# Filler products in five places of TensorE, one value product moved in the attention loop, one memset moved

## The reference

```python
x = x + L0_xattn(layernorm(x), ctx)   # 16 heads of 16 channels, softmax over the 361 context rows
x = x + L0_ffn(layernorm(x))          # shared FFN plus top-2 of 8 experts, 1024 hidden channels
x = x + L1_xattn(layernorm(x), ctx)   # linear layers with ternary weights and int8 inputs, two attention units
x = x + L1_ffn(layernorm(x))          # gated cell scanned over the 16 batches, then tanh of a product
```

```python
attn = softmax(clip(q @ k.T * scale))
x    = (attn @ v) @ Wo + bo
```

## Time and profile before

| What | us |
|---|---|
| median of 3 runs | 918.67 (918.64 to 931.78) |
| the profiled execution, device time | 917.04 |
| its span, first to last instruction | 915.1 |
| TensorE busy | 775.8 |
| VectorE busy | 702.4 |
| ScalarE busy | 557.9 |
| GpSimd busy | 291.6 |
| mean granted TensorE clock | 0.927 of full |

### The profile page before, as it was taken

One profiled execution on the slowest core, in us unless ns is written; L12 is line 12 of the kernel. 1 busy time (PEld: TensorE's weight loads), 2 busy tenths in 40 slices (PEclk: granted clock), 3 DMA queues, 4 the chain that ended last, 5 costly groups with the idle time before them and its releaser, 6 DMA issues.

```text
span 915.1 us, 21761 instructions
## 1 busy us (share of the span) xinstructions
PE 775.8 (85%) x8198; PEld 584.1 (64%) x8198; DVE 702.4 (77%) x1455; ACT 557.9 (61%) x1156; POOL 291.6 (32%) x256
## 2 busy tenths in 40 slices
PE   3788999999998677899899999996647998869995
PEld 1456666666665464778477777783224886459994
DVE  7767888888888897876667776647886987767766
ACT  6657767677674346543655556646977775763542
POOL 6244544535442524050522220005721221532400
PEclk9789999999999778999999999999558999789997
DMA  6434444445543356242477766532210000200002
GB/s 174 109 75 101 118 100 108 108 107 125 140 106 90 94 189 227 90 128 58 125 200 192 197 194 175 151 89 60 74 37 1 1 1 10 85 0 3 3 1 72
DMA packets 75661, 89.60 MB, mean 98 GB/s; under 512 B 22069, under 2 KB 62276, under 8 KB 75584
## 3 DMA queue, kind: packets, MB, share of 16 engines
q1 hardware_dynamic: 68752, 80.50, 31.9%
q0 software_dynamic: 6144, 7.42, 3.3%
q10 hardware_dynamic: 688, 0.66, 0.3%
HBM read 72.87 MB, written 15.43 MB: 97 GB/s over the span
## 4 chain that ended last, share of the span: by engine, by line
PE 50%; DVE 20%; ACT 9%; issue 8%; POOL 6%; DMA 5%; SPq 1%; DVEq 0%; ACTq 0%; POOLq 0%
PE ps L1213 11%; PE ps L1200 9%; PE ps L575 4%; PE ps L547 3%; PE ps L475 3%; PE ps L528 3%; ACT area L1738 2%; PE ps L377 2%; PE ps L619 2%; PE ps L2298 2%; DVE p L563 2%; PE ps L2309 2%; PE ps L1814 2%; ACT area L1705 1%; DVE m L533 1%
## 5 line engine op out<-in xcount | busy, mean ns | idle before, releaser
L533 DVE TENSOR_REDUCE m<-ps 100x2 f32<-100x722 f32 x128 | 114.9, 899 | 48.1 <-PE ps L528 46.8
L554 ACT ACTIVATE p<-ps 128x800 f32<-128x800 f32 x128 | 106.6, 833 | 47.6 <-PE ps L547 45.7
L1262 ACT ACTIVATE hT<-ps,cols 128x500 f32<-128x500 f32 (+1 forms) x96 | 62.5, 651 | 96.6 <-PE ps L1200 85.8
L563 DVE SCALAR_TENSOR_TENSOR p<-p 128x600 f32<-128x600 f32 x128 | 106.1, 829 | 1.0 <-ACT p L554 1.0
L1213 PE MATMUL ps<-w_h,hT_h 128*125 128x256 f16 (+1 forms) x384 | 104.7, 273 | 1.8 <-DVE x L1309 1.2
L1213 PE MATMUL ps<-w_h,hT_l 128*125 128x256 f16 (+1 forms) x384 | 104.7, 273 | 0.0
L1213 PE MATMUL ps<-w_l,hT_h 128*125 128x256 f16 (+1 forms) x384 | 104.7, 273 | 0.0
L1269 DVE TENSOR_TENSOR hT_l<-hT,hT_h 128x500 f16<-128x500 f32 (+1 forms) x96 | 62.4, 652 | 54.6 <-ACT hT_h L1263 54.3
L1105 POOL DMA_INDIRECT xe<-tokens,slot_of x32 | 44.4, 1387 | 146.3 <-PE ps L1223 99.0
L1200 PE MATMUL ps<-xe_h,w_h 128*128 128x500 f16 (+1 forms) x192 | 71.4, 372 | 16.0 <-ACT hT_h L1263 6.2
L1200 PE MATMUL ps<-xe_l,w_h 128*128 128x500 f16 (+1 forms) x192 | 71.1, 370 | 0.0
(11 more groups left out here) (356 smaller groups left out, 2099.7 us busy)
## 6 DMA issues: line engine op xcount, KB each, us to landing
stage<-in_ctxT_dram SPq DMA_DIRECT2D x16, 541.5 KB, 6.2
sw<-in_L_ffn_w_dram SPq DMA_DIRECT2D x16, 512.0 KB
sw<-in_L_ffn_w_dram SPq DMA_DIRECT2D x8, 1024.0 KB, 5.9
k_parts<-kp SPq DMA_DIRECT2D x32, 192.0 KB, 3.9
ks<-k_parts SPq DMA_DIRECT2D x32, 192.0 KB
stage<-in_L_xattn_W_f_dram SPq DMA_DIRECT2D x6, 1024.0 KB, 7.7
ctx_f<-in_ctxT_dram SPq DMA_DIRECT2D x16, 270.8 KB, 3.1
ks<-k_parts SPq DMA_DIRECT2D x32, 96.0 KB
```

What stands on the lines that cost most here:

```text
L533: v.tensor_reduce(m32[p][:, 2 * i:2 * i + 2], ps[0:T, at:at + 2, 0:KV], AX.X, ALU.max).then_inc(m_max, 1)
L554: s.activation(p32[:, i % HALF, :, :, :].rearrange("p j n t -> p n j t"), ps[:, t_bank(i):t_bank(i) + 2, 0:(KJ + 1) * T].rearrange("p n (j ...
L563: v.scalar_tensor_tensor(probs, probs, 1.0, low, ALU.min, ALU.max).then_inc(a_cv, 1)
L1262: s.activation(hT[:, f % 3, 0:m], bank[2 + f % 2][:, 0:m], ACT.Silu, bias=bias, scale=1.0 / WS)
```

## The change

A new function issues n products into a PSUM bank that nobody reads before the next product starts it afresh. It is called in five places: ahead of the first key product; ahead of block f = 2 of the first hidden layer; after the turned layer norm of the third sublayer; after its attention units; and between F1 and F2. In the attention loop, `v_tensor` of step 1 goes ahead of the wait for `m_l` and of `pv_tensor(b - 1, q, 3)`, and `pv_tensor(b, p, 1)` with its wait goes from step 5 to step 6. In the opening, the memset of rows 64 to 127 of the key tile goes behind the first layer norm, and SyncE stores the first keys before it waits for that memset.

```diff
+        def keep_running(pe, at, weights, moving, n):
+            for i in range(n):
+                pe.matmul(at[:, 0:moving.shape[1]], weights, moving, start=True, stop=True)
...
+                if i == 1 and has(b, 2):
+                    v_tensor(pe, b + 1, q, 0, (k_32, 2 * b + 5))
                 if i == 1:
                     pe.wait_ge(m_l, 2 * b + 2)
                 if i == 1 and from_(b, 1):
                     pv_tensor(pe, b - 1, q, NQ - 1)
-                if i == 1 and has(b, 2):
-                    v_tensor(pe, b + 1, q, 0, (k_32, 2 * b + 5))
...
-                if i == 5 and has(b, 1):
+                if i == 6 and has(b, 1):
                     pe.wait_ge(m_l, 2 * b + 3)
-                if i == 5:
+                if i == 6:
                     pv_tensor(pe, b, p, 1)
...
             ln_tensor(pe, 2)
+            pe.wait_ge(ln_ev, 2 * (B // 2) + 1)
+            keep_running(pe, bank[0], w_q[F1][:, 0, 0:128], w_q[F1][:, 1, 0:512], 10)
...
             att_tensor(pe, 1)
+            keep_running(pe, bank[2], w_q[F1][:, 0, 0:128], w_q[F1][:, 1, 0:512], 18)
...
+            pe.wait_ge(h_ev, 8 + 4 * FC - 7)
+            keep_running(pe, bank[0], w_q[F1][:, 0, 0:128], w_q[F1][:, 1, 0:512], 20)
             pe.wait_ge(h_ev, 8 + 4 * FC)
             y2_tensor(pe, 0)
...
-            v.memset(ks_flat[0][64:128, :].bitcast(F32), 0.0).then_inc(k_pad, 1)
             v.memset(floor_k[:, :].bitcast(F32), 0.0).then_inc(k_pad, 1)
             split_weight(v, "Wk")
             open_stats(v, 0)
             open_norm(v, 0)
+            v.memset(ks_flat[0][64:128, :].bitcast(F32), 0.0).then_inc(k_pad, 1)
             split_weight(v, "Wq")
...
+            pe.wait_ge(c_h, 2)
+            keep_running(pe, bank[2], ctxp[0][0][:, 0, 0:128], ctxp[0][0][:, 1, :], 12)
             pe.wait_ge(w_sp, 1)
...
+                if f == 2:
+                    keep_running(pe, bank[4], w1p[0][:, 0, 0:128], xep[0][0][:, 1, 0:GT], 14)
                 hidden_tensor(pe, 0, 0, f)
...
+            for c in range(CC):
+                k_store(sp, 0, 0, 0, c)
             sp.wait_ge(k_pad, 3)
             sp.dma_start(floor_k[ROW_M:128, :], a["pick_h"][:, H * AP:]).then_inc(floor_in, 16)
-            for c in range(CC):
-                k_store(sp, 0, 0, 0, c)
```

## The result

The changed kernel takes 935.2 us against 919.2 (medians of 20 runs each; ratio 1.0169, 95% interval 1.0146 to 1.0193), so it is 15.5 us slower (13.4 to 17.7). The ratio leaves out the runs more than 1.5% above the fastest of their kernel, three of the 20 of the changed kernel and two of the 20 before. The forecast was 924, +6.5 us on the profiled execution, and its range ended at 929. The profiled execution has a span of 928.2 us, 13.1 more than before.

A forecast was written before the change was run, and what follows sets the result against it. TensorE was taken to hold half the chain, its one large loop wait being for `m_l`. Value product +5.6, projection +1.3, opening -0.4 and fillers 0 gave +6.5 us, so 924 us; range 915 to 929.

The forecast's parts named there:

- All 16 batches have this step: 16 x 0.35: Attention loop: moving the value product to step 6 costs 0.35 us in every batch, +5.6 us in all.
- if a second hand-over or the last batches cost double, +0.6 each: Upper bound for the value product's move in the loop: two extra costs of 0.6 us, up to +9.6 us.
- (b): Sign to look for in the changed profile: at step 1 of the loop TensorE waits for ScalarE's key copy.
- (c): Sign for the opening: the first scores start at most 0.5 us earlier than before.
- the start of the low part of `Wq`, 17.37: Opening: with square root 1.15 us earlier and memset of 2.62 added, this split moves from 15.90 to 17.37.
- (d): Sign between attention units and F1's end: GpSimd's row at 810.66 keeps its distance from the end of the attention units.
- The third: Reason for fillers gaining 0 at F1 and F2: the clock falls within the 2.4 to 2.9 us still left idle.
- (e): Sign at F2: its first 64 products take 9 us or more.
- The first (the exponential does not hold): Loop, step 6: ScalarE reaches the exponential later than 194.82 anyway, so 0.67 us per batch is won; 909 us, chance 0.12.
- the second (clock holds): Third and fifth filler places: full clock holds through the shortened gaps, -3.3 us, giving 921 us; chance 0.15.
- the third and fourth: Loop's two trades cancel, 917 us, chance 0.10; a filler runs at half clock, third place, 928 us, chance 0.08.

## Why the prediction was wrong

- **Value product to step 6.** In a steady batch the mechanism was right, and its price too: 0.35 us forecast, 0.37 and 0.33 in the runs with this move. What failed is "All 16 batches have this step: 16 x 0.35". I read one batch in the middle and multiplied, though the last has neither the next batch's scores nor a wait for `m_l` in it. Twelve middle batches cost 3.8 us; the two first and the two last cost 10.8. At the ends the mechanism is another one, in which the forecast had no term: the move also brings the scores of step 6 and VectorE's work behind them forward, these fall beside GpSimd's operations, and GpSimd's take 4.56 instead of 3.04 us and 8.52 instead of 6.94. In batch 1 the key product waits 2.45 us for GpSimd's queue, TensorE's clock falls in that wait, and the two cost 1.3 and some 3.0 us; in the last batch VectorE stands behind GpSimd for 3.31 us. Which clipping lets GpSimd in was read from traces, and no run changed that alone. The bound "if a second hand-over or the last batches cost double, +0.6 each" was an invented size; the profile had the waits of batches 1 and 2 for GpSimd and the half clock of the last batch in it, and I did not read those stretches. The move cost 14.1 us where my upper bound was 9.6.
- **Value projection.** +1.3 forecast, +1.4 measured, uncertain by 3.4; beside the other move 0.22 to 0.26 per steady batch instead of 0.10. (b) of the list held: TensorE waits there for ScalarE's key copy, 0.5 us at most.
- **Opening.** -0.4 forecast; the scores came 2.4 us later in the trace, so (c) failed, in time +1.3, not clear of 0. The step that failed is the start of the low part of `Wq`, 17.37: it left out the memset's 0.70 (the row of 4.87 shows it) and that the normalising moved 1.6 us earlier, beside GpSimd, for +2.05.
- **Fillers: 0 us**, and 0.2 measured. Two reasons held: GpSimd held the end of F1, its row 35.2 us behind the end of the attention units instead of 35.5, which is (d), and ScalarE's transfer took the gain of the second place. The third held in its effect alone: the clock did fall, but 0.8 us after F1's start and 0.2 after F2's, not in the gap. That F2's first 64 products take 9 us or more, (e), failed: they took 8.83. The first place has no run of its own.
- **Rivals.** The first (the exponential does not hold) is refuted by 184.87; the second (clock holds) came in part, in the trace of the changed kernel 0.7 us in the third place and 0.8 in the fifth, of 3.3, and in the time of the fillers' own run not at all; the third and fourth did not come. None of them was a cost at the ends of the loop.

The sum of the four parts measured, the first filler left out, is 14.1 + 1.4 + 1.3 + 0.2 = 17.0 us against 15.5 for the whole, within their uncertainty.

## What to carry to other kernels

Before multiplying the price of one iteration by the number of iterations, look at the first and the last two in the trace: queues are there in another phase, and the move that cost 0.3 us per batch in the middle cost 10.8 us in four batches. What a move delays is to be followed to every engine behind it, and so is what it brings forward: for VectorE and GpSimd it counts whether they now run at the same time. Filler products pay where the products that follow them are themselves in the chain and nothing else ends later: not in the four places of this change that were measured, but in the last batch, where they gave 3.4 us (0.6 to 6.2).

## What was not expected of the hardware

- Operations of VectorE on SBUF tensors stood behind GpSimd's: 0.18 became 3.31 and 2.33 us, 0.76 became 3.73, four of 0.34 became 3.43 together, each time beside a GpSimd operation, and the first ended within 0.06 us of GpSimd's last. It goes the other way too, 3.04 to 4.56 us on GpSimd. By the Trainium skill, "SBUF — State Buffer", section "SBUF: two separate sides", the two engines share a pair of ports that one of them locks for a whole instruction while the other blocks; of VectorE's operations it counts those in a two-port mode or with two SBUF inputs. By that rule a guard operation that takes the ports waits out GpSimd's, and the trace agrees, with 3.31 us; it waited out two of them, since the second followed the first at once. In which mode it ran no row shows. That GpSimd's row grew by just 1.5 us is the distance from one clipping to the next (62.11 - 60.60); that it gets in behind a clipping was read from where the rows end, 0.7 behind one in three traces.
- The granted clock fell to 1.2 GHz after TensorE had begun F1 again at 2.4 GHz: at 796.7, behind an idle time of 2.93 us and 0.8 us of F1. In the run with the value product alone it fell in the wait of 2.45 us in batch 1, 2.1 us after the wait began (65.02 to 67.09), and not in or behind one of 2.50 us in batch 2.
- The same loop takes 284.9 us from the first scores to the last value product in the trace before, 281.8 in that of the fillers 2 to 5 and 286.7 in that of the memset alone. One trace is thus good to some 3 us over the loop, more than three of the four parts of this change are worth, while single batches repeat closely: batch 14 takes 18.68 to 18.70 us in all eight kernels that leave it as it was.
